# Cross-attention block with experts on one core: first maximum pass moved ahead of the branch, no transposed mask, a growing lead in the first unit, and ten unread matmuls at the start

## What is computed

```python
def split_heads(x):                                   # H = 16 heads of width 8
    return x.reshape(Bq, Sq, H, Dq // H).transpose(0, 2, 1, 3)
Q, K, V = split_heads(q @ W_Q), split_heads(k @ W_K), split_heads(v @ W_V)
score = jnp.einsum('bhqd,bhkd->bhqk', Q, K) / math.sqrt(d_k)
score = jnp.where(mask == 0, jnp.float32(-1000000000.0), score)
attn = jax.nn.softmax(score, axis=-1)
out = jnp.einsum('bhqk,bhkd->bhqd', attn, V)          # then heads side by side, @ W_T
...
x = x + jnp.tanh(g_xattn[0]) * _L0_xattn_ref(_layernorm(x, axis=-1), ctx_1024, ctx_1024, mask, ...)
x = x + jnp.tanh(g_ffn[0]) * _L0_ffn_ref(_layernorm(x, axis=-1), w1, w2, router_w)
```

## Time and profile before

| | us |
|---|---|
| median of 3 runs | 510.06 |
| lowest, highest | 508.51, 514.62 |
| the profiled execution, time | 508.19 |
| its span | 506.4 |
| mean granted TensorE clock, share of full | 0.936 |

### The profile page before, as it was taken

How to read it: one execution, slowest core, us unless ns; L and a number is a source line. 1 busy time by engine, 2 the same in 40 slices (tenths; PEclk the granted TensorE clock), 3 DMA queues, 4 the chain that set the end, 5 groups by cost and what they waited for, 6 DMA issues and landing times.

```text
span 506.4 us, 10031 instructions
## 1 busy us (share of the span) xinstructions
PE 456.9 (90%) x3836; PEld 267.9 (53%) x3836; DVE 362.2 (72%) x773; ACT 270.7 (53%) x555; POOL 96.0 (19%) x209
## 2 busy tenths in 40 slices
PE   4866667999969999999999999999999999999596
PEld 1521223645535554666666546566655566666386
DVE  4557543686846789978788898787888987722376
ACT  3300234466646576665666766656567665667231
POOL 6543097136054011000000200000001000000000
PEclk9865595899998999999999999999999999999799
DMA  7439980360861742121121330302122000000000
GB/s 258 104 82 199 251 220 38 99 146 5 304 135 36 164 83 59 27 57 32 37 51 35 74 79 10 75 13 51 35 58 51 2 1 2 1 2 2 21 1 11
DMA packets 21165, 36.86 MB, mean 73 GB/s; under 512 B 2290, under 2 KB 12991, under 8 KB 20988
## 3 DMA queue, kind: packets, MB, share of 16 engines
q1 hardware_dynamic: 19332, 33.96, 27.9%
q0 software_dynamic: 464, 1.64, 1.4%
q10 hardware_dynamic: 1320, 0.60, 0.5%
HBM read 28.13 MB, written 7.80 MB: 71 GB/s over the span
## 4 chain that ended last, share of the span: by engine, by line
PE 73%; DVE 10%; POOL 6%; DMA 5%; issue 3%; ACT 2%; SPq 0%; POOLq 0%; DVEq 0%; ACTq 0%
PE banks L1017 18%; PE banks L988 18%; PE banks L970 14%; PE banks L1049 10%; PE banks L1057 5%; DMA w<-maskT 3%; PE banks L887 3%; DVE chunk_max L721 3%; DVE chunk_max L736 2%; POOL masked_k L495 2%; DMA queries<-neg_rows 2%; PE banks L893 1%; POOL new_rows L468 1%; DMA xs<-x 1%; PE banks L1107 1%
## 5 line engine op out<-in xcount | busy, mean ns | idle before, releaser
L736 DVE TENSOR_REDUCE chunk_max<-banks 128x1 f32<-128x512 f32 (+1 forms) x378 | 233.8, 662 | 59.8 <-PE banks L970 58.7
L608 ACT ACTIVATE probs<-banks 128x512 f32<-128x512 f32 x384 | 211.4, 600 | 114.6 <-PE banks L988 114.2
L988 PE MATMUL banks<-queries,keys 75*128 75x256 bf16 (+1 forms) x832 | 160.2, 278 | 8.9 <-DMA queries<-neg_rows 8.7
L970 PE MATMUL banks<-keys,queries 72*128 72x65 bf16 (+1 forms) x468 | 144.3, 340 | 7.2 <-ACT probs L608 7.2
L988 PEld LDWEIGHTS banks<-queries,keys 75*128 75x128 bf16 (+1 forms) x832 | 72.8, 101 | 88.1 <-issue 29.3
L1017 PE MATMUL banks<-probs,value_t 128*9 128x256 f32 x1536 | 103.1, 387 | 1.5 <-ACT probs L608 1.5
L1049 PE MATMUL banks<-late,w 128*128 128x256 f32 x256 | 67.5, 392 | 0.0
L1017 PEld LDWEIGHTS banks<-probs,value_t 128*9 128x9 f32 x1536 | 33.0, 90 | 48.3 <-issue 17.7
L970 PEld LDWEIGHTS banks<-keys,queries 72*128 72x128 bf16 x468 | 41.9, 99 | 20.9 <-ACT probs L608 10.0
L1049 PEld LDWEIGHTS banks<-late,w 128*128 128x128 f32 x256 | 47.0, 194 | 10.8 <-issue 5.2
L820 DVE SCALAR_TENSOR_TENSOR late<-late,banks 128x256 f32<-128x256 f32 x64 | 26.8, 419 | 35.6 <-ACT late L628 33.9
(11 more groups left out here) (118 smaller groups left out, 278.5 us busy)
## 6 DMA issues: line engine op xcount, KB each, us to landing
keys<-k_parts SPq DMA_DIRECT2D x48, 300.2 KB
k_parts<-split SPq DMA_DIRECT2D x6, 400.2 KB, 4.7
ctx_in<-ctxT SPq DMA_DIRECT2D x3, 800.5 KB, 14.2
k_parts<-late SPq DMA_DIRECT2D x6, 400.2 KB, 5.2
queries<-q_parts SPq DMA_DIRECT2D x16, 144.0 KB
w<-w1T SPq DMA_DIRECT2D x1, 2048.0 KB, 11.3
q_parts<-q_split SPq DMA_DIRECT2D x9, 192.0 KB, 14.8
w<-mask SPq DMA_DIRECT2D x2, 800.5 KB, 6.6
```

The costliest lines, as they stand in the source:

```text
L608: nc.scalar.activation(probs[:, s % (2 * QH), :], ring[ring_bank["scores", n]][:, :], ACT.Exp, scale=SCALE).then_inc(probs_ready, 1)
L736: nc.vector.reduce_max(dst, src, axis=AX.X).then_inc(chunk_used, 1)
L970: last = nc.tensor.matmul(dst[:, i * CW[c]:(i + 1) * CW[c]], queries[q][0:ROWS, j, t * P:(t + 1) * P], keys[q][0:ROWS, j, c * BANK:c * BAN ...
L988: last = nc.tensor.matmul(dst, keys[q][0:KR, j, t * P:t * P + w], queries[q][0:KR, j, :], start=True, stop=not with_mask)
```

## The change

1. The quads are only those of unit 0 (eight), stand ahead of the branch, and always add the mask (four more bf16 matmuls each). The count of zeros, the rest of the value projection and unit 0's transposes follow them, also ahead of the branch.
2. `masked_keys`, its tile and its input are gone. The copy with a mask now uses the untransposed mask as the stationary operand.
3. `chunks_in` (in place of `chunk_at`) gives the slots of unit 0 one and two chunks in turn until the lead is 12, so unit 1's 26 chunks and the first twelve of unit 2 all run in unit 0: 38 chunks. For unit 0 the negation and its transposes are three slots later.
4. Only the first 256 queries are projected ahead; the other 768 are two pieces at the head of the list of pieces, which has 26 now, seven to a unit. ScalarE copies the values' pieces too. GpSimd waits for VectorE's eight normalised tiles before it starts on the keys.
5. SyncE: `load_keys(0, 0)` no longer waits for the stored queries; `load_unit` is for two units ahead, and the weights are loaded behind it; `begin(3)` holds the stores of batches 2 and 3; batch 1's context is loaded sooner; unit 2's keys wait for unit 0's negative maxima.
6. Ten bf16 matmuls of 512 columns, which nobody reads, stand at TensorE's start.

```diff
-QUADS = [(0, t, c) for t in range(QT) for c in range(CH)] + [(1, 0, c) for c in range(CH - 1)]
-LEAD = QH * (CH - 1)
+QUADS = [(t, c) for t in range(QT) for c in range(CH)]
+QUAD_SET = [(i + 1) % 2 for i in range(len(QUADS))]
+LEAD = 12
+RAMP = 10
+FIRST_LATER = 3
-PIECE_SLOTS = (1, 5, 9, 18, 21, 24)
-PIECES = [(b, kind, i) for b in range(1, B) for kind in "KV" for i in range(CH)]
+PIECE_SLOTS = (1, 5, 9, 12, 18, 21, 24)
+PIECES = [("Q", 0, 0), ("Q", 0, 1)] + [(kind, b, i) for b, kinds in ((1, "VK"), (2, "VK"), (3, "KV"))
+                                       for kind in kinds for i in range(CH)]
...
-    u, i = divmod(n + LEAD, CHUNKS)
-    return (u + 1, i) if u + 1 < B * NQ else None
+def chunks_in(n):
+    first = n + min(LEAD, (n + 1) // 2)
+    last = n + 1 + min(LEAD, (n + 2) // 2)
+    return [g for g in range(first, last) if g < CHUNKS * (B * NQ - 1)]
...
+            sp.dma_start(ctx_in[:, 1, :], ctxT[1]).then_inc(ld_ctx[1], 16)
             sp.wait_ge(k_stored[0], 16 * PARTS)
+            load_keys(0, 0)
             sp.wait_ge(q_stored, 16 * PARTS * PARTS)
-            load_unit(0, 0)
+            load_queries(0, 0)
             load_unit(0, 1)
+            sp.wait_ge(neg_in, 16 * PARTS)
             load_unit(0, 2)
-            sp.wait_ge(q_cut, 8)
+            sp.wait_ge(row_cut, 2)
...
                 if u == 1:
+                    sp.dma_start(ctx_in[:, 0, :], ctxT[2]).then_inc(ld_ctx[2], 16)
+                    load_unit(0, 3)
                     store_keys(1)
...
+                if u == 3:
+                    store_keys(2)
+                    store_keys(3)
+                if u >= 2 and u + 2 < B * NQ:
+                    b, q = divmod(u + 2, NQ)
+                    sp.wait_ge(scores_ready, SLOTS * (u - 1))
...
+                    load_unit(b, q)
                 if u == 2:
-                    store_keys(2)
-                    sp.wait_ge(mask_done, 3)
+                    sp.wait_ge(mask_used, QT)
                     sp.dma_start(w1[:, :, :], w1T.rearrange("d (e i) -> d e i", e=E)).then_inc(ld_fw, 16)
...
-                if 1 <= u and u + 3 < B * NQ:
-                    b, q = divmod(u + 3, NQ)
-                    sp.wait_ge(scores_ready, SLOTS * u)
...
-                    load_unit(b, q)
...
+            pool.wait_ge(xn_ready, B * QT)
             for c in range(CH):
                 cols = slice(c * BANK, c * BANK + CW[c])
                 pool.wait_ge(k_hi, c + 1)
...
             load_values(0, 0)
-            masked_keys()
...
-                        if s == S_NEGATE and more:
+                        if s == neg_slot(u, S_NEGATE) and more:
                             negate(*following(b, q))
...
+            def quad(i):
+                t, c = QUADS[i]
+                hold(pe, quad_used, i - 1)
+                pe.wait_ge(mask_used, t + 1)
+                w = CW[c]
+                for j in range(QH):
+                    rows = slice(32 * j, 32 * (j + 1))
+                    nc.tensor.matmul(bank[QUAD_SET[i] * QH + j][:, 0:w], q_unit[rows, t * P:(t + 1) * P],
+                                     keys32[rows, c * BANK:c * BANK + w], start=True, stop=False)
+                for j in range(QH):
+                    last = nc.tensor.matmul(bank[QUAD_SET[i] * QH + j][:, 0:w], ident_neg[:, :],
+                                            masked_q[:, t, c * BANK:c * BANK + w], start=False, stop=True)
...
+            pe.wait_ge(ident_ready, 3)
+            for _ in range(RAMP):
+                nc.tensor.matmul(xnT_banks[0][:, :].rearrange("p (n c) -> p n c", c=P), ident_b[:, :],
+                                 ident_b[:, None, :].broadcast_to([P, BANK // P, P]), start=True, stop=True)
             pe.wait_ge(ld_wk, 16)
...
+            pe.wait_ge(v_copied, 2)
+            pe.wait_ge(q_unit_ready, 1)
+            for i in range(len(QUADS)):
+                if i == 1:
+                    pe.wait_ge(xnT_copied, 2)
+                    pe.wait_ge(q_rows_ready, 1)
+                quad(i)
+            pe.wait_ge(quad_used, len(QUADS) - 1)
```

377 lines of the change are left out of this document (167 added, 210 removed).

## The result

| | before | after |
|---|---|---|
| median, us | 509.28 (4 runs, 507.70 to 514.62) | 495.36 (4 runs, 493.56 to 497.51) |
| profiled execution / its span, us | 508.19 / 506.4 | 493.56 / 491.8 |
| mean granted clock | 0.936 | 0.969 |

The ratio is 0.971, with a 95% interval of 0.964 to 0.978: the changed kernel is about 3% faster. The forecast was 476, with a range of 467 to 488. The direction was right. The size was not: between the profiled executions 14.6 us came where 32 were expected, and the measured time lies outside the range. The profiled execution of the changed kernel is the fastest of its four.

What follows compares the result with a forecast made beforehand. TensorE, busy 90% of the span, was taken as the bound, with time lost ahead of unit 0, in it and before unit 3. Sum: 41 + 29.5 + 74 + 329.3 = 473.8, plus 1.8 around: 475.6, rounded to 476; range 467 to 488.

Steps and rivals of the forecast that it cites:

- Start to the first quad: From kernel start, through VectorE's eight tiles (2.1 us) and the keys' projection (2.7 us), to the first quad at 15.1 us.
- The rival of quads at the low clock: Ahead of unit 0: the quads run at the low clock, unit 0 starts at 47, time 482 us; chance 0.2.
- Reduction to unit 0: From the last reduction at 33.0 us to unit 0's start at 41: 7.0 until the maxima land, 1 for hand-overs.
- with only unit 1's keys under way (below) I take 2: Ahead of unit 0: negative maxima land 2 us after issue, against 7.7 before, since only unit 1's keys share the queues.
- Unit 0: The first unit takes 29.5 us in place of 40.2, including 2.1 lost to the low clock at its start; gain 10.7.
- The term of 13.8 us for the transposed mask: In unit 0: removing the transposed mask saves TensorE's 6.64 us wait and 7.2 us lost to the low clock behind it.
- The rival of a slow unit 0: Unit 0's clock stays low, costing 5 us, or nine query stores block unit 1's maxima; time 481 to 482; chance 0.2.
- Units 1 to 3: These three units together take 74.0 us in place of 79.0, a gain of 5.0.
- the term for the weights: At unit 3: issuing weights in unit 1's last third removes a 3.96 us wait and 1.8 of low clock; gain 5.7.
- I count no stall, and 3 us as the bad end: In unit 3: unit 5's keys, queued behind two stores and wanted ten slots later, cause no wait, at worst 3 us.
- the last rival: From unit 2 on, twelve loads with a shorter lead stall and make the kernel slower than before, for example 524; chance 0.01.
- The ten matmuls: At the start: rival that they fail to raise the projections' clock; first quad at 20, start 52, time 487; chance 0.1.

## Why the prediction was wrong, step by step

*Start to the first quad*: right, 15.04 for 15.1, with 2.13 for VectorE's eight tiles and 3.08 for the keys' projection. The first comparison of the mask took 1.56 us beside GpSimd, the second 1.01, against 0.94 each in the kernel before, where GpSimd was idle beside most of them; the copy that the first quad waits for stood behind the first one, and TensorE was idle 0.29 us for it. So what the prediction left in the range for them, about 1 us each, came to 0.3 at most. The Trainium skill, page "SBUF — State Buffer", section "Who interferes with whom", lets a VectorE operation in a two-port mode and a GpSimd operation exclude each other; the eight tiles, 4.67 us beside GpSimd and 2.13 alone, agree with it. The two comparisons agree only in part: GpSimd was at work beside both, and one of them lost next to nothing. *The quads*: full clock was right but for one; the last reduction was at 34.9 for 33.0. The rival of quads at the low clock was true for 3.3 us behind the short quad, after TensorE had stood 1.62 us. This varies between executions: of the eight profiled ones with this order of the quads, five had VectorE idle 3.1 to 3.5 us there and ended at 34.7 to 35.1, and three had it idle 1.87, as before the change, and ended at 33.5. The Trainium skill, page "TensorE: Matmul & The Clock Gate", section "A second HAM failure mode: psum-queue depth-cycling", which the prediction cited, tells of a clock that swings in a kernel cycling through banks with short idle times. Little of that is seen here: beside idle times of 0.16 to 0.34 us the quads kept the full clock, and the granted clock fell once, from 24.0 to 27.3, behind the longer stop.

*Reduction to unit 0*: wrong, 12.1 us for 8.0, which is 4.1 of the 6.0 us of this stage; the quads have the other 1.9. The step that failed is "with only unit 1's keys under way (below) I take 2". The maxima took 6.3 us after their last issue. Two terms under that step were wrong. The first is the landing of the stored queries, 31.5: the 2.1 us of the earlier trace rows were for queues with little else in them (the engines were busy 0.13 to 0.41 of the time then), and here the context and unit 0's keys, which the change itself had moved ahead, were in the queues, so it took 7.1 us. By the prediction's times unit 1's load, issued then, was through by 38.5, as the maxima went out; in fact it was issued from 37.33, just ahead of them. The second is the load, 1.04 MB: 9.5 us from its first issue until the maxima had landed, and not 6. Windows of it:

```profile
37.30:38.30 1.00, 0.50 (x4) 0.19 (x2) 0.00 (x0) 0.81 (x2) 0.00 (x0) 1.00 0.11 32
38.30:45.30 7.00, 0.00 (x0) 0.00 (x0) 0.00 (x0) 0.26 (x1) 0.65 (x2) 0.70 0.81 168
45.30:46.90 1.60, 0.00 (x0) 0.00 (x0) 0.00 (x0) 0.00 (x0) 0.00 (x0) 0.50 0.21 32
```

While it moved, the rate was near the 181 GB/s of the earlier trace rows that the prediction used. What a rate alone leaves out is the microsecond at its start and the 1.6 at its end, in which the engines were nearly idle, 2.6 us together. With the maxima ahead of the keys they landed in 1.1 us, and with the context away the stores were 2.5 us sooner.

*Unit 0*: 30.4 for 29.5. The term of 13.8 us for the transposed mask is borne out by taking the mask out of the kernel before, which made unit 0 13.1 us shorter. The twelve more chunks and the denser pieces can be read off the unit at full clock, 28.2 to 28.6 us in three kernels; my sum gave 27.4. What the start at the low clock adds I put at 2.1; the profiles show 1.8 in the changed kernel and up to 8 in others. The rival of a slow unit 0 through a clock that stays low, priced at 5 us, did not come in this profile; it did in those of two other kernels whose unit 0 does the same work (34.9 and 36.8 us).

*Units 1 to 3*: the term for the weights was exact (unit 3 starts without a wait, and 5.7 us in the kernel before with the weights later), unit 1 was right, unit 2 has a wait of 1.70 us that I hadn't looked for: GpSimd's splits of the pieces stand ahead of its negation. The large error is the sentence "I count no stall, and 3 us as the bad end" on unit 5's load. Its own numbers gave more: the 2.2 MB that the sentence names, at the 145 GB/s that I used for the last rival, are 15 us, and ten slots of 0.95 are 9.5, so a stall of 5.7. In the trace the stores began at 135.51, some 2 us later than I had them, the load was issued until 140.8 and landed at 150.2: 14.7 us from the first issue. With the low clock behind the wait it cost 10.3 us in this stage, more than half of the miss, and one moved line takes it out of unit 3.

*The rest*: 329.7 for 329.3, right. *The ten matmuls*: the rival priced their failure at 487, from a first quad at 20. Without them that quad starts at 15.21. The projection took 4.38 us then, between the 5.31 of before and the 3.08 with them, and the last reduction ended at 33.5: this rival was no danger, and the ten matmuls no gain.

So every removal was sized well: GpSimd beside VectorE, the transposed mask, the weights. What was sized badly, in both places, is what the moved transfers met in their new place.

## What to carry to other kernels

When a change moves transfers to an earlier place in a queue, write down for the whole stretch how many bytes are in front of each small transfer that something waits for, and where the DMA engines have little to do because the queue holds the next load back behind a landing. At the start of this kernel three 2 KB transfers landed 1.1 or 6.3 us after their last issue by what stood before them, and for the same bytes the order cost 3.7 and 4.6 us where it left the engines little to do, and 1.5 where it didn't. When a load is queued behind a store, its lead begins when the store's producer is done, not at its own slot. And an idle TensorE costs twice, for the wait and for the low clock behind it, so unread matmuls are worth their time only where it is idle anyway: thirteen that ended with the load gained 4 us or somewhat more (unit 0 took 28.6 us for 32.8, and started at the same time), 24 gained nothing, and 34 lost some 8 by the ratios (4 by the medians).

## What the runs showed that I had not expected

The rise of the clock at the start of unit 0 varied between executions by as much as the effects under study: in one it stayed at the low level (1.2 GHz) for 16.5 us in which TensorE was busy throughout, while the changed kernel's unit 0 had a mean of 0.93 over all its 30.4 us. In the kernel with thirteen unread matmuls, and in that with 24, it was up when they ended. The times of the kernel without them spread over 6.3 us, with thirteen over 4.5 and with 24 over 1.8 (six runs each), which is too few to call the matmuls the cause. What sets the moment of the rise stays open.

Where TensorE reads the count and enters the code of the branch it stands 2.4 to 4.2 us in which it waits for nothing that the trace shows (the "issue" idle ahead of the unread matmuls: 2.38, 3.31 and 4.23 in three kernels). No run separates the read from the branch. That time is hidden here only because the load is later.

The maxima are issued on ScalarE's queue and unit 1's load on SyncE's, and yet the maxima (2.0 KB each, three of them) landed 6.3 us after their last issue with that load under way and 1.1 us after it without. The Trainium skill, page "DMA: Bandwidth & Descriptors", section "Queues, rings and completion order", says that a DMA engine takes turns between its queues, a packet at a time. From that I would have expected a small transfer on a queue of its own to pass a large one. The measurement decides here: it waited for most of the load. It did not always wait for all of it: in the kernel with the negation first the maxima had landed at 46.18, and TensorE waited 1.41 us more for the load, until 48.49.
